# Two attention layers with experts: score products in 32-row tiles, and a last pass with filler products

## The reference

```python
x = _layernorm(x + _L0_attn_ref(x, ...))   # 16 heads of 8, rotary positions
x = _layernorm(x + _L0_ffn_ref(x, ...))    # 8 experts, each takes its 256 best tokens
x = _layernorm(x + _L1_attn_ref(x, ...))   # keys and values from a latent of 32
x = _layernorm(x + _L1_ffn_ref(x, ...))    # 16 experts, each token takes its 4 best
```

## Time and profile before

| | before |
|---|---|
| median of 3 runs | 691.19 us (688.80 to 692.06) |
| the profiled execution: its time | 691.12 us |
| its span, first to last instruction | 689.3 us |
| TensorE busy, share of the span | 540.6 us, 78% |
| VectorE busy | 493.6 us, 72% |
| ScalarE busy | 385.9 us, 56% |
| GpSimd busy | 326.8 us, 47% |
| mean granted TensorE clock | 0.882 of full |

### The profile page before, as it was taken

The page is one execution under the profiler, slowest core; times in us unless marked ns, Lnnn a source line. Parts: engine busy times, 40 slices in busy tenths (PEclk is TensorE's granted clock), DMA queues, the critical chain, the costliest instruction groups (busy, mean ns, idle before and its releaser), DMA issues.

```text
span 689.3 us, 15558 instructions
## 1 busy us (share of the span) xinstructions
PE 540.6 (78%) x4528; PEld 388.7 (56%) x4528; DVE 493.6 (72%) x1779; ACT 385.9 (56%) x1004; POOL 326.8 (47%) x431
## 2 busy tenths in 40 slices
PE   4769999998512895378999999823899999999960
PEld 2224555555301785244555555512777899999960
DVE  6788888995576421868888899587577778863257
ACT  2348888886200564256888888530344555566633
POOL 5665555505001577562333330734344677777630
PEclk9689999999755799589999999955799999999985
DMA  6502080001100125336404000103334455555572
GB/s 185 160 1 71 9 232 24 1 1 41 26 0 3 39 49 101 122 94 178 136 11 123 1 2 1 47 16 105 119 126 136 156 185 177 177 194 203 199 249 77
DMA packets 64437, 65.08 MB, mean 94 GB/s; under 512 B 16115, under 2 KB 45955, under 8 KB 63846
## 3 DMA queue, kind: packets, MB, share of 16 engines
q1 hardware_dynamic: 57094, 52.49, 23.9%
q0 software_dynamic: 7264, 11.62, 6.9%
HBM read 29.77 MB, written 11.87 MB: 60 GB/s over the span
## 4 chain that ended last, share of the span: by engine, by line
PE 58%; DVE 22%; issue 6%; DMA 4%; POOL 4%; SPq 3%; ACT 2%; DVEq 0%; ACTq 0%; POOLq 0%
PE bank L1285 10%; PE bank L1296 9%; PE bank L898 8%; PE bank L865 8%; PE bank L881 7%; DVE mx L1687 2%; DVE passed L1887 2%; PE bank L915 2%; PE bank L1239 2%; PE bank L1080 1%; POOL rstd L711 1%; POOL sum L766 1%; PE bank L1266 1%; DVE keys L1737 1%; DVE stats L1831 1%
## 5 line engine op out<-in xcount | busy, mean ns | idle before, releaser
L1687 DVE TENSOR_REDUCE mx<-bank 128x2 f32<-128x512 f32 x256 | 166.2, 686 | 32.2 <-PE bank L865 29.3
L1406 ACT ACTIVATE prob<-bank 128x512 f32<-128x512 f32 x256 | 141.4, 597 | 45.4 <-PE bank L881 34.7
L1587 ACT ACTIVATE queries<-bank,prob 128x128 f32<-128x128 f32 x316 | 90.1, 368 | 81.3 <-PE bank L1285 80.5
L865 PE MATMUL bank<-keys,queries 128*128 128x512 f16 x256 | 99.3, 402 | 9.6 <-DVE queries L1747 4.0
L1285 PE MATMUL bank<-keys,prob 128*128 x632 | 90.0, 287 | 3.8 <-ACT keys L1579 3.7
L881 PE MATMUL bank<-QT,keys 128*128 128x256 f16 x512 | 90.3, 276 | 0.0
L1296 PE MATMUL bank<-W,queries 128*128 x632 | 87.8, 283 | 0.0
L1285 PEld LDWEIGHTS bank<-keys,prob 128*128 128x128 f32 x632 | 79.7, 198 | 8.8 <-issue 7.0
L779 POOL DMA_INDIRECT prob<-xs,idx_g x64 | 61.5, 961 | 46.4 <-DVE idx_g L2118 27.8
L1296 PEld LDWEIGHTS bank<-W,queries 128*128 128x128 f32 x632 | 77.6, 193 | 2.0
L898 PE MATMUL bank<-prob,augs 128*32 128x256 f32 x1024 | 77.2, 389 | 0.0
(11 more groups left out here) (272 smaller groups left out, 1021.4 us busy)
## 6 DMA issues: line engine op xcount, KB each, us to landing
prob<-W SPq DMA_DIRECT2D x79, 258.0 KB
W<-in_w SPq DMA_DIRECT2D x48, 256.0 KB, 3.5
sum<-zero SPq DMA_DIRECT2D x3, 1024.0 KB, 8.8
xr<-XT SPq DMA_DIRECT2D x12, 128.0 KB, 2.0
xs<-X SPq DMA_DIRECT2D x2, 768.0 KB, 6.2
prob<-xs,idx_g POOLq DMA_INDIRECT x80, 2.7
XB<-sum SPq DMA_DIRECT2D x1, 1024.0 KB, 5.3
Y<-sum SPq DMA_DIRECT2D x4, 256.0 KB, 4.8
```

Of the source, the lines that this page charges most:

```text
L865: nc.tensor.matmul(bank[S1B[u % 2]][:, :], QT[par][:, j, P * qt:P * qt + P], KB[par][:, j, 2 * qp:2 * qp + 2, :], start=True, stop=True).t ...
L1406: nc.scalar.activation(prob[:, v % 8, :, :], st_bank(b, v)[:, :], ACT.Exp, scale=SCALE).then_inc(exp_done, 1)
L1587: last = nc.scalar.activation(hid2[:, p % 4, f, :], bank[2 + p % 2][:, P * f:P * f + P], ACT.Gelu, bias=wc[:, p % 4, WB + f:WB + f + 1])
L1687: nc.vector.tensor_reduce(m_at, bank[S1B[u % 2]][:, :].rearrange("p (j k) -> p j k", j=2), AX.X, ALU.max).then_inc(s1_used, 1)
```

## The change

- **Score tiles.** The keys are kept as `keyT`, without the zeros. Each score product uses the 32 rows of its own head alone. A unit of `s1` is now two products of 256 columns (two heads with the same `q`, from blocks `2*jp` and `2*jp + 1`), a unit of `st` still two of 256. Neighbouring units have another `q`, so other rows. The tables of the order differ, the projections' second half comes at unit 7, and the query transposes go before the key transposes.
- **Key copies.** ScalarE fills `keyT` with two copies of 128 rows per batch; VectorE's copies and GpSimd's clearing are gone.
- **Last batch's second pass.** It is written out in another order, with `hold` in two places: 10 and 4 products of constants (bf16, 256 columns) into a free half of bank 5, whose result nobody reads.
- **Expert steps.** The expert's number is computed once per pair and used for the slot and for the second product. `row_owned` sums eight tiles' row numbers in one reduction rather than one tile's in each.
- **Final sums.** The bank sums and the first slices come before the third slice.
- Statistics of an output batch are taken at the end of the pass instead of in the next.

```diff
@@ -54,14 +54,8 @@
...
 def soft_units(u):
...
-    return {2: [0, 1], 3: [2], 4: [3], 5: [4], 6: [5], 7: [6], 8: [7], 9: [8], 10: [9], 12: [10, 11],
-            14: [12], 15: [13]}.get(u, [])
...
-def soft_units_alone(u):
...
-    return {1: [0, 1], 2: [2], 3: [3], 4: [4], 5: [5, 6], 6: [7], 7: [8], 8: [9], 9: [10, 11], 10: [12], 11: [13],
-            12: [14], 13: [15]}.get(u, [])
+    return {2: [0], 3: [2], 4: [3], 6: [4, 5], 7: [6], 8: [7], 9: [8], 10: [9], 11: [10], 12: [11],
+            14: [12, 13]}.get(u, [])
@@ -146,7 +140,7 @@
...
         keys = sb("keys", [P, RING * P])
-        KB = [keys[:, 2048 * i:2048 * i + 2048].bitcast(F16).rearrange("p (j q l) -> p j q l", j=NJ, q=4) for i in range(2)]
+        keyT = [keys[:, 512 * i:512 * i + 512].bitcast(F16).rearrange("p (j l) -> p j l", j=NJ) for i in range(2)]
         QT2 = sb("QT2", [P, NJ, L], F16)
...
-                nc.gpsimd.memset(KB[i][:, :, :, :].bitcast(I32), 0)
                 last = nc.gpsimd.memset(vaug[i][:, :, :, HD:HD + 1], 1.0)
@@ -854,21 +845,24 @@
             def s1(lay, i, par, u):
...
                 g = i + NB * lay
-                qt, j, qp = u // 8, (u % 8) // 2, u % 2
+                qt, jp, q = u // 8, (u % 8) // 4, u % 4
+                rows = slice(HP * q, HP * q + HP)
                 if u == 0:
...
                 if u in (0, 4):
-                    pe.wait_ge(kb_act, 2 * g + u // 4 + 1)
-                    pe.wait_ge(kb_dve, 2 * g + u // 4 + 1)
+                    pe.wait_ge(kt_ready, 2 * g + u // 4 + 1)
                 if not (isinstance(i, int) and g == 0 and u < 2):
                     pe.wait_ge(s1_used, 16 * g + u - 1)
-                nc.tensor.matmul(bank[S1B[u % 2]][:, :], QT[par][:, j, P * qt:P * qt + P],
-                                 KB[par][:, j, 2 * qp:2 * qp + 2, :], start=True, stop=True).then_inc(s1_done, 1)
+                for j in range(2):
+                    last = nc.tensor.matmul(bank[S1B[u % 2]][:, L * j:L * j + L], QT[par][rows, 2 * jp + j, P * qt:P * qt + P],
+                                            keyT[par][rows, 2 * jp + j, :], start=True, stop=True)
+                last.then_inc(s1_done, 1)
...
             def st(lay, b, par, v):
...
                 j, q = v // 4, v % 4
+                rows = slice(HP * q, HP * q + HP)
                 if v in (0, 8):
@@ -879,7 +873,7 @@
...
                     last = nc.tensor.matmul(st_bank(b, v)[:, L * kt:L * kt + L],
-                                            KB[par][:, j, q, P * kt:P * kt + P], QT2[:, j, :],
+                                            keyT[par][rows, j, P * kt:P * kt + P], QT2[rows, j, :],
                                             start=True, stop=True)
@@ -949,77 +943,96 @@
...
                     st(lay, i - 2, par, 15)
-                    bt(lay, i - 2, 0)
                 for u in range(16):
                     s1(lay, i, par, u)
+                    if u == 1 and tail_on:
+                        bt(lay, i - 2, 0)
                     if u == 1 and soft_on:
...
                         av(lay, i - 2, par, 3, 0)
-                    if u == 3 and tail_on:
-                        av(lay, i - 2, par, 3, 1)
+                    if u == 3 and soft_on:
+                        st(lay, i - 1, nxt, 1)
                     if joined and u == 0:
...
                         front_latent(lay, i + 2, par)
+                    if u == 3 and tail_on:
+                        av(lay, i - 2, par, 3, 1)
                     if u == 5 + late and proj_on:
...
                         av(lay, i - 1, nxt, 0, u // 9)
-                    if u == 10 and tail_on:
+                    if u == 7 + late and proj_on:
+                        front_proj(lay, i + 2, par, 1)
+                    if u in (10, 12) and soft_on:
+                        av(lay, i - 1, nxt, 1, u // 12)
+                    if u == 13 and tail_on:
                         out_transposes(lay, i - 2)
-                    if u == 11 and soft_on:
-                        av(lay, i - 1, nxt, 1, 0)
                     if u == 13 and front_on:
-                        key_transposes(lay, i + 1, nxt)
-                    if u == 13 and soft_on:
-                        av(lay, i - 1, nxt, 1, 1)
+                        query_transposes(lay, i + 1, nxt)
                     if u == 15 and tail_on:
...
                     if u == 15 and front_on:
-                        query_transposes(lay, i + 1, nxt)
+                        key_transposes(lay, i + 1, nxt)
                     if soft_on:
...
                             st(lay, i - 1, nxt, v)
-                    if u == 12 and proj_on:
-                        front_proj(lay, i + 2, par, 1)
                     if u == 15 and soft_on:
...
+            def hold(lay, n):
...
+                pe.wait_ge(tq2_ready, 2 * (NB - 1 + NB * lay) + 2)
+                for _ in range(n):
+                    nc.tensor.matmul(bank[M5][:, 2 * P:4 * P], ones_b[:, :], bsplit[:, 0:2 * P], start=True, stop=True)
...
             def pe_last_soft(lay):
...
                 i, par, nxt = NB, 0, 1
...
+                b, c = NB - 2, NB - 1
+                st(lay, b, par, 14)
+                st(lay, b, par, 15)
+                bt(lay, b, 0)
+                max_transposes(lay, i, nxt)
+                av(lay, b, par, 2, 1)
+                av(lay, b, par, 3, 0)
+                av(lay, b, par, 3, 1)
+                for v in range(4):
+                    st(lay, c, nxt, v)
+                tail_turns(lay, i, 2)
+                hold(lay, 10)
+                bt(lay, b, 1)
+                st(lay, c, nxt, 4)
+                st(lay, c, nxt, 5)
+                hold(lay, 4)
+                av(lay, c, nxt, 0, 0)
+                st(lay, c, nxt, 6)
+                av(lay, c, nxt, 0, 1)
+                st(lay, c, nxt, 7)
+                out_transposes(lay, b)
+                st(lay, c, nxt, 8)
+                tail_turns(lay, i, 7)
+                st(lay, c, nxt, 9)
+                out_product(lay, b)
+                av(lay, c, nxt, 1, 0)
+                st(lay, c, nxt, 10)
+                av(lay, c, nxt, 1, 1)
+                st(lay, c, nxt, 11)
+                tail_turns(lay, i, 10)
+                st(lay, c, nxt, 12)
+                st(lay, c, nxt, 13)
+                tail_turns(lay, i, 13)
+                bt(lay, c, 0)
+                av(lay, c, nxt, 2, 0)
+                st(lay, c, nxt, 14)
+                av(lay, c, nxt, 2, 1)
+                st(lay, c, nxt, 15)
@@ -1497,12 +1510,8 @@
...
                     act.wait_ge(st_done, 16 * (g - 2) + 8 * pair + 8)
-                for q in range(2):
-                    rows, js = slice(HP * q, HP * q + HP), slice(2 * pair, 2 * pair + 2)
-                    last = nc.scalar.copy(KB[par][rows, js, q, :],
-                                          half[M6][rows, 2 * L * pair:2 * L * pair + 2 * L].rearrange(
-                                              "p (j k) -> p j k", j=2))
-                last.then_inc(kb_act, 1)
+                nc.scalar.copy(keyT[par][:, 2 * pair:2 * pair + 2, :],
+                               half[M6][:, 2 * L * pair:2 * L * pair + 2 * L]).then_inc(kt_ready, 1)
...
             def front_evac(lay, b, par, t):
@@ -1681,20 +1690,16 @@
...
                 for u in range(16):
-                    qt, h = u // 8, 2 * (u % 8)
+                    qt, jp, q = u // 8, (u % 8) // 4, u % 4
                     dve.wait_ge(s1_done, 16 * g + u + 1)
-                    m_at = mx[:, qt, h:h + 2]
+                    m_at = mx[:, qt, :].rearrange("p (j q) -> p j q", q=4)[:, 2 * jp:2 * jp + 2, q]
                     nc.vector.tensor_reduce(m_at, bank[S1B[u % 2]][:, :].rearrange("p (j k) -> p j k", j=2), AX.X,
...
                         norm(lay, i - 2, 1)
-                    if u == 11 and i > 2:
-                        output_statistics(lay, i - 3)
                     if u == 13 and front_on:
-                        keys_evac(lay, i + 1, nxt, 0)
-                    if u == 15 and front_on:
                         q_evac(lay, i + 1, nxt)
@@ -1706,13 +1711,12 @@
...
                                         ALU.subtract).then_inc(m_ready, 1)
-                if front_on:
-                    keys_evac(lay, i + 1, nxt, 1)
+                if tail_on:
+                    output_statistics(lay, i - 2)
@@ -2008,21 +1999,25 @@
...
                 dve.wait_ge(slice_back[0], 16)
-                for k in range(1, TOPK - 1):
-                    dve.wait_ge(slice_back[k], 16)
-                    for c in range(4):
-                        at = slice(4 * c, 4 * c + 4)
-                        last = nc.vector.tensor_tensor(Y[:, at, :], Y[:, at, :], slice_of[k][:, at, :], ALU.add)
-                    step(last)
+                dve.wait_ge(slice_back[1], 16)
                 for c in range(4):
                     at = slice(4 * c, 4 * c + 4)
-                    last = nc.vector.tensor_tensor(X[:, at, :], X[:, at, :], Y[:, at, :], ALU.add)
```

(19 more changed lines are left out.)

100 lines of the change are left out of this document (28 added, 72 removed).

## The result

The changed kernel takes **647.27 us** (median of four runs, 644.81 to 651.17) against 691.26 for the kernel before beside it: ratio 0.9375, 95% interval 0.932 to 0.943. Forecast were 680.6 us, with a range of 669 to 702. The direction was right, the size was not: -44 us in place of -10.5. The profiled execution is the slowest of the four (651.17 us, span 649.4). Ratios leave out runs over 1.5% above the fastest of their kernel, since some executions fall into a slower state.

The account below looks back on a forecast made before the run. No engine's busy share named the bound; in steady attention passes TensorE, VectorE and ScalarE were near their limit. Terms -13.2 - 2 + 10 - 2 - 1 - 2.3 = -10.5 from 691.12 gave 680.6 us, range 669 to 702.

Parts of the forecast that it names:

- Score tiles, steady passes: Attention layers: overlapping score products and fewer VectorE copies shorten the period by 1.65 to 15.7 us; eight periods, -13.2 us.
- The floor of 14.7: Steady passes: VectorE's sixteen maxima, 0.65 us apart, and 4.4 us of other work as lower bound of the period.
- Rival 2: Steady passes: score-bank ping-pong with VectorE's maxima, or ScalarE's exponentials, holds the period at 16.8; 692 us; chance 0.16.
- rival 4: Score products: row groups don't overlap, period 18.3 us, low-clock pass 27 us; 714 us in all; chance 0.10.
- Passes without projections: Four attention passes that project nothing: VectorE at the same floor, -0.5 us each, -2 together.
- Clock: Second passes of both layers: 32-row scores keep TensorE's clock low through that pass; +10 us together, bounds 0 and +20.
- Rival 1: Second passes: the clock rises as before, as if rows didn't count; the +10 goes, 670.6 us; chance 0.12.
- Rival 3: Attention layers: clock low one more pass per layer, or falling in a steady pass; 700.6 us, long tail; chance 0.15.
- Last second pass: Last batch's second pass: fourteen fillers hidden in waits, reordering gives ScalarE work; -1 us per layer, -2 together.
- Expert steps: Expert pairs: shared number gains nothing, reductions fall from 64 to 8, mostly hidden behind TensorE; -1 us.
- Final sums: End of kernel: bank sums fill VectorE's 2.35 us wait and the last slice is used last; -2.3 us.
- Start: Kernel start: the dropped clearing of the keys, 3.8 us on POOL, ends before anyone waits for it; 0 us.

Follow-up runs that it names:

- 128-row kernel: The changed kernel with every score product over all 128 rows in the same places; median 740.12 us, ratio to the kernel before 0.984.
- rows 0 to 31: The changed kernel with every score product on the same 32 rows, so neighbours share a row group; four runs between 778 and 806 us.

## Why the prediction was right or wrong

In the profiled executions the change is -39.9 us where the sum has -10.5. Three terms carry most of the 29.4 us between them: the low clock in the second passes (+10 forecast, -1.1 measured), the expert steps (-1 and -13.4) and the steady passes (-13.2 and -22.6). The last second passes (-2 and +7.2) hid 9 us of it.

**Score tiles, steady passes: right in kind, mis-sized.** The step said that a stretch of n units costs (n + 1) x 0.107, since the next unit overlaps by one. This law failed: four units run side by side (eight products in 0.34 us with the border). Overlap alone gives 2.1 us a pass against 128 rows in the same order (layer 0). From 142.60 to 143.58 the 128-row kernel needs 0.98 us for what takes 0.34 here, 2.9 times. VectorE's copies, counted with the two on the chain (0.86), are worth all four once TensorE is shorter (1.7). The floor of 14.7, given as a bound, was nearly the measured value: VectorE still has 1.6 us of gaps, but 14.59 follows each microsecond added to it. Rival 2, another floor at 16.8, and rival 4 did not come.

**Passes without projections.** "-0.5 each" failed: 2.0 or 1.8, and 0.8. In the first of each pair both savings count: it is 15.1 us with all 128 rows and 15.3 with VectorE's copies back, against 13.47. The second has no key copies, and the added ones leave it at 12.87; there the overlap alone gives 1.0 (13.88 with all rows).

**Clock.** The step was right that with few-row products the clock rises later, at 45.8 and 305.3 us: in layer 0 7.8 us after the pass's start, where it was 3.5 before the change. "Through that pass" was too long, it was half of it. Rival 1, "as if rows didn't count", is refuted by the pair of 128 and 32 rows (full from 43 us, long times until 68). The share of time that TensorE is busy does not, taken alone, tell the two apart: in layer 1's second pass it is 97% with all rows, at a clock of 1.00, and over 99% with rows 0 to 31, at 0.50. The price was wrong: 22 us for that pass, measured 16.9 from the transposes at 37.98 to the value products at 54.84. I priced the scores with the failed (n + 1) law at the low level, and the whole pass at it, while the level lasted for 7.8 us. Against the second passes with fillers ahead of them the low clock costs 2.1 and 2.3 us. Rival 3 showed only in the kernel with rows 0 to 31.

**Last second pass.** "Hidden" fits the fillers' own cost, but missed their worth, 7 us in the one set that shows it, most likely by the clock (0.832 to 0.853 over the span with them, 0.816 to 0.839 without). The -1 per layer came out as +1.4 and +5.8. In layer 1 the clock fell 14 us into the stage (411 us), before the change 22 us into it. In layer 0 it fell after 23.0 us, before the change after 23.8, so the clock doesn't explain the +1.4. The new order also has a wait of 0.69 us for ScalarE ahead of the last value products, which the old one had not; how much of the +1.4 that is was not tried.

**Expert steps: the largest miss.** "From 520 us on TensorE is the bound" and "twelve lie on VectorE's path" fell. Before, VectorE is on the chain of waits again and again until about 540 us, and the first twenty pairs take 61.0 us; now 52.2. What goes per pair on VectorE is one gap of 0.41 us and some one and a half reductions of 0.17. I counted the register instructions and found them equal; I did not ask what they stand behind. The edit alone shortens the pairs by 14.1 us.

**Final sums: right**, -2.4 alone. Faster pairs took 1.7 of it back, since the scatters became last; the stage is 0.7 shorter.

**Start.** The dropped clearing is worth 0, as said. I had missed that the moved projection also moves GpSimd's large addition, beside which VectorE's small operations take longer (in the changed kernel 2.48 us in place of 0.18 for one; before the change 4.47 in place of 0.24 for a cast): 3.7 us by that move. The start is only 3.2 earlier than before the change; what costs the other 0.5 is open.

## What to carry to other kernels

For instructions whose address is computed, ask what the register work stands behind, not how much there is: here a wait ahead of it went with an idle 0.41 us a pair. If two engines are near the same limit, price an edit that relieves both as a pair, since each half alone looks small (here 0.7 to 1.1 us a pass alone, 2.9 together). Products on few rows left the TensorE clock low for longer after a pause here (from 38 us, where TensorE had waited 3.9, 2.7 and 1.9 us, until 43 with all rows in use, 45.8 with four row groups in turn and about 68 with one group); with full-array fillers in that pause, where nobody waits for TensorE, the second passes were 2.1 and 2.3 us shorter in one profile and 0.6 and 2.8 in another.

## What was not expected of the hardware

- Products of four 32-row groups start within 0.02 us though each group's second product is queued between them.
- From the same low level at 38 us, with the same columns and order, the clock was full from 43 us with score products on 128 rows, and products took their long times (0.60 us for two score products, 0.39 after) until about 68 us with all of them on the same 32 rows; in layer 1 the clock there stayed at 0.50 for some 60 us, from 329 to 388, in which TensorE was idle for 0.14 us.
- A 32-row stretch paid 0.09 us at a border to transposes (0.31 against 0.22 us for two products); 128-row scores paid nothing there.
- A VectorE cast of 32 columns took 4.47 us beside a GpSimd addition of 4.49 us, and 0.24 elsewhere.
